# Latent attention in a macaron transformer kernel: the value products of a pair in two runs, with a ring of ten places for the exponents

## Chip, cores and metric

One Trainium2 chip (trn2), one core of it. The metric is the device time of the whole program in microseconds (us), as the median of several runs. All data are float32.

## What is computed

Input x has 4 batch elements of 1024 tokens with 128 channels. Six blocks follow each other, each on the layer norm of x and added to it: a mixture of experts (half weight), a causal attention with a polynomial in place of the softmax, the mixture of experts again, a feed-forward block with token-dependent weights, the latent attention, and the feed-forward block again. Only the latent attention is touched by the change. Cut to what matters:

```python
def _L1_attn_ref(x, latent_w, latent_b, Wd_w, Wd_b, out_w, out_b):
    b, t, c = x.shape                       # 4, 1024, 128
    Wdkv = x @ latent_w + latent_b          # keys and values alike, 36 wide
    q = jnp.einsum('btc,hcl->bhtl', x, Wd_w) + Wd_b[None, :, None, :]   # 16 heads
    scores = jnp.einsum('bhtl,bsl->bhts', q, Wdkv) / np.sqrt(8)
    scores = jnp.where(causal, scores, -jnp.inf)
    attn = jax.nn.softmax(scores, axis=-1)
    y = jnp.einsum('bhts,bsl->bhtl', attn, Wdkv)
    z = jnp.transpose(y, (0, 2, 1, 3)).reshape(b, t, h * 36)
    return z @ out_w + out_b
```

## The kernel before, in words

The function `attn1_phase` (from L1671) holds the latent attention. Each engine runs its own program, and semaphores alone order them against each other. `pipeline` (in each program: `start`, then four elements of eight `pair` calls and one `finish`) sets the order: an element is a batch element, a pair is two of the sixteen heads, m counts pairs over all elements, i counts them in an element, and q is i modulo 2. The first three elements run in a hardware loop with `more` true, the last one behind it with `more` false.

**Two passes over the scores.** The softmax needs the maximum of each row before the exponent. So the scores of a pair are computed twice. One pair ahead, `scores_max` (L1959) computes them with queries as rows, in sixteen blocks of 128 queries: eight wide ones (1024, 896, 768 or 640 keys) that all go to the same two PSUM banks, and eight narrow ones (512 keys or fewer) that all go to the third. VectorE's `maximum` (L2277) adds the causal mask to a block and takes the maximum of its rows; a small read instruction then ends it. Before TensorE writes a bank again it waits for the maximum of the block that lay there. The sixteen are dealt to slots 0 to 7 of TensorE's order (`MAXIMA`): one wide block in each, with narrow ones beside it. `transpose_max` (L1965) turns the sixteen maxima, ScalarE and VectorE split them in a high and a low part, and SP writes both to the query matrix with a small DMA each. Then the real `scores` (L1974) of the next pair, with keys as rows, can start: they wait for these DMAs (`m_in`).

**Units.** The real scores of a pair are computed in units. A unit holds for both heads (c = 0 and 1) a piece of 128 keys by up to 512 queries, or several smaller pieces. There are ten units, NU = 10: 0, 1 and 2 lie on the diagonal of the second half of the queries, 3 to 6 are full pieces of that half, 7, 8 and 9 are the diagonal of the first half. Units 0, 3 to 6 and 7 have 512 columns, 1 and 8 have 384 and 128, 2 and 9 have 256. A score matmul pair goes to one of three PSUM banks, ScalarE takes the exponent (L2174) into the tensor `probs`, GpSimd zeroes what lies above the diagonal in units 0, 1, 2, 7, 8 and 9 (L1886), and TensorE multiplies with the values (`values`, L1990) and adds up in one of two banks, one for each half of the queries. The value matmuls use 64 columns of the array for each head, so that both heads run side by side. `copy_out` on ScalarE (L2162) copies a finished half away.

**The ring.** `probs` has RING = 4 places of 1024 columns. Unit u of a pair lies at place (u + 2q) modulo 4 (`ring`, L1766). ScalarE's `exponent` waits ahead of a unit until the unit that lay four before in the order is multiplied (`pv_ready`, m * NU + u - RING).

**TensorE's order in a pair** is written by hand (L2033 to L2068), in STEPS = 5 steps d = 0 to 4. Each step has slot 2d - 1 of the maxima (from d = 1), three scores, slot 2d (up to d = 3), a fourth score, and then a run of value products: at d = 0 those of units 8 and 9 of the pair in front (if it belongs to the same element), at d = 1 units 0 and 1, at d = 2 units 2 and 3, at d = 3 units 4 and 5, at d = 4 units 6 and 7. At d = 4 the transpose of the maxima and `project` (the queries of the pair three further, L1943) stand ahead of the values. The last pair of an element has units 8 and 9 right behind 6 and 7. All of this is one queue: what stands behind a waiting instruction waits too.

**Special pairs.** Pair i = 5 (OPENS) of the first three elements transposes the next element's x in place of the projection. Pair i = 6, the opening pair, computes the next element's latents ahead of its first score, and at d = 0, behind the value products, projects queries (`project(m + 2, 0)`), for which ScalarE and VectorE then make the high and low parts, before slot 0 of the maxima. In the last element only pairs 0 to 4 project, and the last pair has no maxima.

**ScalarE's order in a pair** (`pair` at L2168 and on): the exponents of units 0 to 9, with `copy_out` of the second half of the pair in front behind unit 1, and in the opening pair `high_query` behind that; after the units the high part of the next queries, and the copy of the first half.

The order in the queues of SP and GpSimd is by `s_ready` (scores done), `qs_ready` and `p_ready` (exponents done); the change has no line there but for `ring`, which GpSimd's `causal_part` uses too.

Of the kernel before, what the change touches and what calls it, by code (L numbers as in the profile page):

```python
# [34 lines left out]
def after(n):  # L35

    return n + 1 + LEAD
# [1633 lines left out]
def attn1_phase(nc, t, tag):  # L1671


    with ExitStack() as ctx:
        def sb(name, shape, dt=F32):
            return ctx.enter_context(nc.sbuf_tensor(f"{tag}_{name}", shape, dt))
# [23 lines left out]
        ml = sb("ml", [16, 2, P], F32R)  # L1700
        probs = sb("probs", [P, RING, 2, HALF])
        yT = sb("yT", [P, PAIRS, SEQ])
# [31 lines left out]
        NU, NE = len(units), 2 * len(units)  # L1734
# [3 lines left out]
        STEPS = NU // 2  # L1738
# [26 lines left out]

        def ring(q, u):  # L1766

            return (u + 2 * q) % RING

        def o_part(j, rows, n):  # L1770

# [33 lines left out]
        def follows(i, k, more):  # L1805

            return more or i + k < PAIRS
# [5 lines left out]
        with nc.Block() as block:  # L1813
# [97 lines left out]
            def _(pe):  # L1911
# [35 lines left out]
                def scores_max(m, q, n, keys, spare=False):  # L1947
                    c, j = IN_ORDER[n]
                    before = bank_before(n, spare)
                    if not of_kind(n) and j >= 4:  # L1950
                        pe.wait_ge(q_in[q][0], (m - q) * 48 + 96)
                    elif not of_kind(n):
                        pe.wait_ge(q_in[q][1], (m - q) * 24 + 48)
                        pe.wait_ge(q_first[q], (m - q) * 24 + 48)
                    if before >= 0:
                        pe.wait_ge(mx_ready, after(m * 16 + before))
                    for lo in range(0, (j + 1) * P, HALF):
                        hi = min(lo + HALF, (j + 1) * P)
                        last = pe.matmul(max_part(n, lo, hi, spare), qS[q][0:STACK, c, j * P:(j + 1) * P], keys[0:STACK, lo:hi],  # L1959
                                         start=True, stop=True)  # L1960
                    last.then_inc(sm_ready, 1)

                def transpose_max(m, q):
                    pe.wait_ge(mx_ready, after(m * 16 + 15))
                    pe.transpose(o_part(0, 16, P), mx[:, q, :], t.ident).then_inc(mt_ready, 1)  # L1965
# [12 lines left out]
                def values(m, q, u):  # L1978
                    h = 0 if u < N1 else 1
                    pieces = units[u][1]  # L1980
                    first, end = u in (0, N1), u in (N1 - 1, NU - 1)
                    if first:
                        pe.wait_ge(yc_ready, after((m - 1) * 2 + h))
                    if u in DIAGONAL:
                        pe.wait_ge(tri_ready, after(m * len(DIAGONAL) + DIAGONAL.index(u)))
                    else:
                        pe.wait_ge(p_ready, after(m * NE + 2 * u + 1))
                    for k, (kt, at_, qc, n, _) in enumerate(pieces):
                        for c in range(2):
                            last = pe.matmul(y_bank[h][VW * c:VW * (c + 1), qc:qc + n], V[:, kt, :], probs[:, ring(q, u), c, at_:at_ + n],  # L1990
                                             start=first and k == 0, stop=end, skip_group_check=True)
                    last.then_inc(pv_ready, 1)
# [19 lines left out]
                def pair(m, i, b, more):  # L2012
                    q = i % 2
                    ahead = follows(i, 1, more)
                    opening = more and i == OPENS + 1
                    keys = kN if i == PAIRS - 1 else kS

                    def maximum(k):
                        if not ahead:
                            return  # L2020
                        if k == 0:
                            if follows(i, 2, more):
                                pe.wait_ge(qs_ready, after((m + 2) * 2 + 1))
                            pe.wait_ge(ml_ready, after(m))
                            if opening:
                                pe.wait_ge(v_ready, after(b + 1))
                        if k == 1 and i == 0:
                            pe.wait_ge(res.xo_ready, after(b * BT - 1))
                        for n in range(FIRST[k], FIRST[k + 1]):
                            scores_max(m + 1, 1 - q, n, keys)  # L2030

                    for d in range(STEPS):
                        if d == 0 and opening:  # L2033
                            latents(b + 1)
                        if d >= 1:
                            maximum(2 * d - 1)
                        for u, c in ((2 * d, 0), (2 * d, 1), (2 * d + 1, 0)):
                            scores(m, q, u, c)
                        if d == 0 and opening:
                            pe.wait_ge(ml_ready, after(m))  # L2040
                            latent_rows(b + 1)
                        if d < STEPS - 1 and not (d == 0 and opening):
                            maximum(2 * d)
                        scores(m, q, 2 * d + 1, 1)
                        if d == STEPS - 1:
                            if ahead:
                                transpose_max(m + 1, 1 - q)
                            if more and i == OPENS:
                                transpose_x(b + 1)
                            if projected(i, more):  # L2050
                                project(m + 3, (i + 3) % PAIRS)
                        if d == 0:
                            if i > 0:
                                for u in (NU - 2, NU - 1):
                                    values(m - 1, 1 - q, u)
                            if opening:
                                pe.wait_ge(ks_ready, after(b * 2 + 3))
                                project(m + 2, 0)
                                maximum(0)
                        else:  # L2060
                            for u in (2 * d - 2, 2 * d - 1):
                                values(m, q, u)
                    if i == PAIRS - 1:
                        for u in (NU - 2, NU - 1):
                            values(m, q, u)
# [47 lines left out]
            def _(act):  # L2113
# [44 lines left out]
                def copy_out(m, i, h):  # L2158
                    s = HALVES[h]
                    act.wait_ge(pv_ready, after(m * NU + (NU if h else N1) - 1))  # L2160
                    act.sem_inc(act_pause, 1)
                    act.activation(yT[:, i, s * HALF:(s + 1) * HALF], y_bank[h], ACT.Copy).then_inc(yc_ready, 1)  # L2162

                def pair(m, i, b, more):
                    q = i % 2
                    opening = more and i == OPENS + 1

                    def exponent(u, c):  # L2168
                        k = 2 * u + c
                        act.wait_ge(s_ready, after(m * NE + k))  # L2170
                        if c == 0:
                            act.wait_ge(pv_ready, after(m * NU + u - RING))
                        n = 256 if len(units[u][1]) == 1 and units[u][1][0][3] == 256 else HALF
                        act.activation(probs[:, ring(q, u), c, HALF - n:HALF], e_part(k, HALF - n, HALF), ACT.Exp,  # L2174
                                       scale=SCORE_SCALE).then_inc(p_ready, 1)

                    if opening:
                        low_keys(b + 1)
                    for u in range(NU):
                        exponent(u, 0)  # L2180
                        if u == NU - 1 and follows(i, 1, more):
                            high_max(m + 1, 1 - q)
                        exponent(u, 1)
                        if u == 1:
                            if i > 0:
                                copy_out(m - 1, i - 1, 1)
                            if opening:
                                high_query(m + 2, 0, True)
                    if more and i == OPENS:
                        high_x(b + 1)  # L2190
                    if projected(i, more):
                        high_query(m + 3, (i + 3) % PAIRS, True)
                    copy_out(m, i, 0)
                    if i == PAIRS - 1:
                        copy_out(m, i, 1)
# [125 lines left out]
        sem.end()  # L2321


RING = 4
OPENS = PAIRS - 3


# [127 lines left out]
```

## Time and profile before

| | us |
|---|---|
| median of 3 runs | 3007.7 (3005.54 to 3011.52) |
| the profiled execution, its time | 3009.96 |
| its span in the trace | 3008.2 |
| TensorE matmul busy | 2717.3 (90%) |
| VectorE busy | 1908.3 (63%) |
| ScalarE busy | 1136.8 (38%) |
| GpSimd busy | 924.1 (31%) |
| mean granted TensorE clock | 0.937 of full speed |

Busy time is the union of an engine's instruction spans, and matmul ends are modelled, so a TensorE that is busy in the table is not one at its peak. The latent attention fills the span from about 2010 to 2915 us; an ordinary pair takes about 23 us of it.

### The profile page before, as it was taken

The page shows a single profiled execution, that of the slowest core. Times are in us where ns is not written, and L with a number is a line of the kernel's source. Part 1 is how long each engine was busy: PE and PEld are TensorE (multiplying, and loading weights), DVE is VectorE, ACT ScalarE, POOL GpSimd, SP SyncE. Part 2 cuts the span into 40 slices and gives each one's busy share as a digit, 9 for nine tenths or more (in the row PEclk, how much of TensorE's full clock was granted, in tenths as well). Part 3 has the DMA queues.
Part 4 walks back from the last instruction along what each step waited for, and adds up shares of the span by engine and source line. Part 5 has one row for each costly group of instructions (what it writes and reads, how often), then busy time and mean ns, then how long its engine had stood idle before and what let it go on. Part 6 is the DMA issues. An engine that isn't in the chain of part 4 may idle for free. (4 is left out here: it accounts for less than half of the span.)

```text
span 3008.2 us, 53420 instructions
## 1 busy us (share of the span) xinstructions
PE 2717.3 (90%) x15208; PEld 1878.1 (62%) x15208; DVE 1908.3 (63%) x5011; ACT 1136.8 (38%) x2101; POOL 924.1 (31%) x1235
## 2 busy tenths in 40 slices
PE   6999999968888888789999999778998998998989
PEld 5888888845555555468888888434455455455454
DVE  6777777746665666477777777445555555555542
ACT  3111111116666667521111111234544544544544
POOL 3222233216666666542222222001111211211200
PEclk9999999968898898889999999888999999999999
DMA  4000000000000000110000000001111111111100
GB/s 138 0 0 0 0 0 0 0 1 2 2 3 3 3 3 3 36 67 0 0 0 0 0 0 1 1 21 28 43 31 28 43 30 28 43 29 31 43 2 28
DMA packets 31963, 51.87 MB, mean 17 GB/s; under 512 B 8178, under 2 KB 14066, under 8 KB 31732
## 3 DMA queue, kind: packets, MB, share of 16 engines
q1 hardware_dynamic: 27124, 41.88, 4.6%
q0 software_dynamic: 4608, 7.09, 0.9%
q8 instruction: 124, 2.03, 0.3%
q14 instruction: 107, 0.88, 0.1%
HBM read 17.93 MB, written 2.10 MB: 7 GB/s over the span
## 5 line engine op out<-in xcount | busy, mean ns | idle before, releaser
L640 DVE SCALAR_TENSOR_TENSOR moe_acc<-moe_ps,moe_comb,moe_acc 128x512 f32<-128x512 f32 x896 | 660.9, 744 | 154.5 <-PE moe_ps L346 151.5
L2277 DVE CUSTOM_DVE_ANT_0 attn_masked<-attn_psm,attn_causal 128x1024 f32<-128x1024 f32 (+1 forms) x504 | 363.2, 757 | 260.4 <-PE attn_psm L1959 259.7
L2174 ACT ACTIVATE attn_probs<-attn_pse 128x512 f32<-128x512 f32 (+1 forms) x640 | 313.6, 556 | 342.4 <-PE attn_pse L1974 339.8
L377 PE MATMUL moe_ps<-moe_Wd,moe_ih 128*128 128x512 f32 x1024 | 344.1, 418 | 4.6 <-DVE moe_Wd L563 4.6
L346 PE MATMUL moe_ps<-moe_Wg,moe_xh 128*128 128x512 f32 x1024 | 328.9, 403 | 16.9 <-DVE moe_Wg L563 16.9
L346 PE MATMUL moe_ps<-moe_Wu,moe_xh 128*128 128x512 f32 x1024 | 334.1, 408 | 2.7 <-POOL moe_Wu L501 2.7
L1886 POOL TENSOR_SCALAR_AFFINE_SELECT attn_probs<-attn_probs 128x256 f32<-128x256 f32 (+1 forms) x192 | 95.1, 496 | 711.9 <-ACT attn_probs L2174 711.8
L1990 PE MATMUL attn_psy<-attn_probs,attn_V 128*64 128x512 f32 (+3 forms) x1536 | 291.4, 510 | 0.0
L511 POOL TENSOR_SCALAR moe_part<-consts,moe_pick,moe_prob 128x8 f32<-128x8 f32 x256 | 97.9, 400 | 626.9 <-ACT moe_prob L434 626.9
L1959 PE MATMUL attn_psm<-attn_kS,attn_qS 108*128 108x512 f32 (+3 forms) x672 | 197.8, 395 | 49.9 <-DVE attn_mx L2277 43.9
L1145 POOL TENSOR_TENSOR attn_R<-attn_R 128x1024 f32<-128x1024 f32 (+1 forms) x128 | 213.9, 1681 | 92.5 <-DVE attn_R L1511 91.7
L346 PEld LDWEIGHTS moe_ps<-moe_Wg,moe_xh 128*128 128x128 f32 x1024 | 195.2, 192 | 65.7 <-issue 20.8
L1974 PE MATMUL attn_pse<-attn_qS,attn_kS 110*128 110x512 f32 (+3 forms) x768 | 207.5, 366 | 23.3 <-ACT attn_probs L2174 10.3
L346 PEld LDWEIGHTS moe_ps<-moe_Wu,moe_xh 128*128 128x128 f32 x1024 | 191.3, 192 | 47.0 <-issue 5.4
L1959 PEld LDWEIGHTS attn_psm<-attn_kS,attn_qS 108*128 108x128 f32 x672 | 112.5, 195 | 168.0 <-DVE attn_mx L2277 147.4
L433 ACT ACTIVATE moe_prob<-moe_gap 128x2 f32<-128x2 f32 x64 | 13.0, 203 | 519.4 <-DVE moe_gap L631 519.4
L377 PEld LDWEIGHTS moe_ps<-moe_Wd,moe_ih 128*128 128x128 f32 x1024 | 182.8, 193 | 41.0 <-issue 4.8
L346 PE MATMUL moe_ps<-moe_Wg,moe_xl 128*128 128x512 f32 x512 | 205.2, 401 | 0.0
L346 PE MATMUL moe_ps<-moe_Wu,moe_xl 128*128 128x512 f32 x512 | 204.8, 400 | 0.0
L377 PE MATMUL moe_ps<-moe_Wd,moe_il 128*128 128x512 f32 x512 | 203.6, 398 | 0.0
L1511 DVE TENSOR_SCALAR attn_R<-attn_e 128x1024 f32<-128x1024 f32 (+1 forms) x128 | 139.2, 1087 | 92.9 <-PE attn_e L1210 87.1
L1990 PEld LDWEIGHTS attn_psy<-attn_probs,attn_V 128*64 128x64 f32 x1536 | 97.0, 140 | 134.7 <-issue 122.9
(233 smaller groups left out, 4686.9 us busy)
## 6 DMA issues: line engine op xcount, KB each, us to landing
attn_qS<-attn_qH SPq DMA_DIRECT2D x192, 72.0 KB
attn_qS<-attn_qL SPq DMA_DIRECT2D x96, 72.0 KB
attn_qS<-attn_qH POOLq DMA_DIRECT2D x64, 72.0 KB, 2.0
moe_stageg<-in_w_gate SPq DMA_DIRECT2D x8, 512.0 KB, 7.2
moe_stageu<-in_w_up SPq DMA_DIRECT2D x8, 512.0 KB, 7.4
moe_stageg<-in_w_down SPq DMA_DIRECT2D x8, 512.0 KB, 4.0
attn_qS<-attn_qL POOLq DMA_DIRECT2D x32, 72.0 KB, 2.5
out<-X SPq DMA_DIRECT2D x8, 256.0 KB, 2.4
```

The source lines that it names most:

```text
L346: last = pe.matmul(expert_bank[j % 4][:, :], a[q][:, :], w[b][:, cols], start=k == 0, stop=k == 2)
L377: last = pe.matmul(y_bank[h][:, :], a[q][:, rows], W[2][b][:, cols], start=c == 0 and k == 0, stop=c == KC - 1 and k == 2)
L511: ins = pool.tensor_scalar(part[:, q, r, k, :], t.iota8, pick[:, q, r, k:k + 1], prob[:, q, r, k:k + 1], ALU.is_equal, ALU.mult)
L640: dve.scalar_tensor_tensor(acc[:, q, r, :], expert_bank[j % 4][:, :], comb[:, q, r, e:e + 1], acc[:, q, r, :], ALU.mult, ALU.add).then_inc ...
L1145: pool.tensor_tensor(r, r, r, ALU.mult).then_inc(sq01_ready, 1)
L1511: dve.tensor_scalar(R[:, r, 0:2, HALF - n:HALF], e01[u % 2][:, :, HALF - n:HALF], LIFT, -HALF_LIFT, ALU.max, ALU.add).then_inc(read01, 1)
L1886: pool.affine_select(some, some, [[0, 2], [0, (hi - lo) // P], [1, P]], ALU.is_ge, nothing, base=0, channel_multiplier=-1).then_inc(tri_re ...
L1959: last = pe.matmul(max_part(n, lo, hi, spare), qS[q][0:STACK, c, j * P:(j + 1) * P], keys[0:STACK, lo:hi], start=True, stop=True)
L1974: last = pe.matmul(e_part(k, at_, at_ + n), kS[:, kt * P:(kt + 1) * P], qS[q][:, c, s * HALF + qc:s * HALF + qc + n], start=True, stop=True)
L1990: last = pe.matmul(y_bank[h][VW * c:VW * (c + 1), qc:qc + n], V[:, kt, :], probs[:, ring(q, u), c, at_:at_ + n], start=first and k == 0, s ...
L2174: act.activation(probs[:, ring(q, u), c, HALF - n:HALF], e_part(k, HALF - n, HALF), ACT.Exp, scale=SCORE_SCALE).then_inc(p_ready, 1)
L2277: dve.tensor_tensor_reduce(masked[:, 0 if j >= 4 else 1, 0:n], max_part(k, 0, n, spare), causal[:, SEQ - n:SEQ], 1.0, NEG, ALU.add, ALU.ma ...
```

## The change

The value products of a pair come in two runs. The first, at d = 1, has units 8 and 9 of the pair in front and then units 0 and 1. The second, at the end of d = 4, has units 2 to 7. Steps 0, 2 and 3 have none. The last pair of an element still has units 8 and 9 at its end. Since exponents now wait longer for their product, the ring has ten places, one for each unit, and a unit lies at the place of its own number. On ScalarE the copy of the second half of the pair in front moves from behind unit 1 to behind unit 3.

```diff
         def ring(q, u):
 
-            return (u + 2 * q) % RING
+            return u
...
-                        if d == 0:
+                        if d == 1:
                             if i > 0:
                                 for u in (NU - 2, NU - 1):
                                     values(m - 1, 1 - q, u)
+                            for u in range(2):
+                                values(m, q, u)
+                        if d == STEPS - 1:
+                            for u in range(2, NU - 2):
+                                values(m, q, u)
+                        if d == 0:
                             if opening:
                                 pe.wait_ge(ks_ready, after(b * 2 + 3))
                                 project(m + 2, 0)
                                 maximum(0)
-                        else:
-                            for u in (2 * d - 2, 2 * d - 1):
-                                values(m, q, u)
...
                         exponent(u, 1)
+                        if u == 3 and i > 0:
+                            copy_out(m - 1, i - 1, 1)
                         if u == 1:
-                            if i > 0:
-                                copy_out(m - 1, i - 1, 1)
                             if opening:
                                 high_query(m + 2, 0, True)
...
-RING = 4
+RING = 10
```

## Rows read from the trace of the kernel before

In the order of time the columns are: start us, us, engine, line, operation, output<-inputs, xcount, and in brackets the idle time before it and its releaser; instructions of a kind are merged, and overlapping groups may start before the one in front ends. In the stretches the columns are: start:end, length, busy us (xcount) of PE, PEld, DVE, ACT and POOL, granted clock, DMA share, GB/s.

**Rows 1.** The order of time, TensorE, one ordinary pair (columns as above).

```profile
2337.80 0.96 PE L1974 MATMUL attn_pse<-attn_qS,attn_kS 110*128 110x512 f32 x4 [0.17 <-DMA attn_qS<-attn_ml]
...
2339.50 1.51 PE L1990 MATMUL attn_psy<-attn_probs,attn_V 128*64 128x384 f32 x12
2340.95 0.84 PE L1959 MATMUL attn_psm<-attn_kS,attn_qS 108*128 108x512 f32 x3
...
2342.80 1.12 PE L1959 MATMUL attn_psm<-attn_kS,attn_qS 108*128 108x512 f32 x3 [0.55 <-DVE attn_mx L2277]
...
2347.24 0.44 PE L1959 MATMUL attn_psm<-attn_kS,attn_qS 108*128 108x384 f32 x1 [0.49 <-DVE attn_mx L2277]
2347.51 0.87 PE L1974 MATMUL attn_pse<-attn_qS,attn_kS 110*128 110x512 f32 x3
2348.22 0.76 PE L1959 MATMUL attn_psm<-attn_kS,attn_qS 108*128 108x512 f32 x3
2348.82 0.39 PE L1974 MATMUL attn_pse<-attn_qS,attn_kS 110*128 110x512 f32 x1
2349.14 1.51 PE L1990 MATMUL attn_psy<-attn_probs,attn_V 128*64 128x256 f32 x8
2350.58 0.73 PE L1959 MATMUL attn_psm<-attn_kS,attn_qS 108*128 108x512 f32 x3
...
2352.24 0.73 PE L1959 MATMUL attn_psm<-attn_kS,attn_qS 108*128 108x512 f32 x3 [0.22 <-DVE attn_mx L2277]
...
2353.18 1.94 PE L1990 MATMUL attn_psy<-attn_probs,attn_V 128*64 128x512 f32 x8
2355.05 0.67 PE L1959 MATMUL attn_psm<-attn_kS,attn_qS 108*128 108x512 f32 x3
...
2356.77 0.38 PE L1974 MATMUL attn_pse<-attn_qS,attn_kS 110*128 110x256 f32 x1 [0.31 <-ACT attn_probs L2174]
...
2358.89 1.94 PE L1990 MATMUL attn_psy<-attn_probs,attn_V 128*64 128x512 f32 x8
2361.17 0.96 PE L1974 MATMUL attn_pse<-attn_qS,attn_kS 110*128 110x512 f32 x4 [0.34 <-DMA attn_qS<-attn_ml]
```

**Rows 2.** The same stretch, VectorE: the reads that end four wide maxima.

```profile
2340.69 0.08 DVE L2277 DVE_READ_ACCUMULATOR2_ANT attn_mx<- 128x1 f32 x1
...
2350.02 0.08 DVE L2277 DVE_READ_ACCUMULATOR2_ANT attn_mx<- 128x1 f32 x1
...
2352.10 0.08 DVE L2277 DVE_READ_ACCUMULATOR2_ANT attn_mx<- 128x1 f32 x1
...
2354.15 0.08 DVE L2277 DVE_READ_ACCUMULATOR2_ANT attn_mx<- 128x1 f32 x1
```

**Rows 3.** The order of time, TensorE: an opening pair and a first pair.

```profile
2193.22 0.71 PE L1959 MATMUL attn_psm<-attn_kS,attn_qS 108*128 108x512 f32 x2 [1.88 <-DVE attn_qL L2253]
2195.50 0.84 PE L1959 MATMUL attn_psm<-attn_kS,attn_qS 108*128 108x512 f32 x3 [1.57 <-DVE attn_mx L2277]
...
2270.82 1.43 PE L1959 MATMUL attn_psm<-attn_kS,attn_qS 108*128 108x512 f32 x3 [1.55 <-DVE attn_mx L2277]
```

**Rows 4.** The same view: the run at the end of an element.

```profile
2238.63 3.23 PE L1990 MATMUL attn_psy<-attn_probs,attn_V 128*64 128x512 f32 x20
2241.80 1.09 PE L2079 MATMUL attn_psm<-consts,attn_yT 128*128 128x128 f32 x8
```

**Rows 5.** The order of time, TensorE: the last element, starts of pairs 6 and 7.

```profile
2852.21 0.96 PE L1974 MATMUL attn_pse<-attn_qS,attn_kS 110*128 110x512 f32 x4 [1.17 <-DMA attn_qS<-attn_ml]
...
2875.77 0.96 PE L1974 MATMUL attn_pse<-attn_qS,attn_kS 110*128 110x512 f32 x4 [2.12 <-DMA attn_qS<-attn_ml]
```

**Rows 6.** Stretches: the opening pairs of the first two elements.

```profile
2184.52:2217.81 33.29, 28.35 (x134) 15.75 (x133) 16.63 (x40) 14.85 (x29) 4.49 (x9) 0.90 0.09 25
2408.26:2443.14 34.88, 29.99 (x134) 16.65 (x133) 16.64 (x40) 14.88 (x29) 4.49 (x9) 0.85 0.09 24
```

**Rows 7.** The order of time, ScalarE, in the pair of rows 1.

```profile
2348.03 2.06 ACT L2174 ACTIVATE attn_probs<-attn_pse 128x512 f32<-128x512 f32 x4 [3.25 <-PE attn_pse L1974]
```

## The prediction

> **What bounds the kernel now.** I read the attention part of the second layer, since the diff touches nothing else. I went first to the order of time on TensorE, pair by pair, then to VectorE in the same stretch, then to the stretches with their granted clock. One pair of heads is the stretch from its first score matmul to that of the next, 2337.80 to 2361.17, 23.37 us [rows 1]. Within it TensorE never stands for long. Its marked waits are 0.55 and 0.49 and 0.22 us (for VectorE's maxima), 0.31 (an exponent) and 0.34 (the DMA of the low part of the maxima) [rows 1]. So TensorE's stream sets the end, but only because of how it is interleaved. Slot after slot it writes a block of masked scores for the next pair into the one wide bank, VectorE takes its maximum, and TensorE must not write the wide bank again until VectorE has read it. The value products (L1990) are what TensorE does in the meantime: five runs, at d = 0 to 4. Three of them lie exactly on such a wait [rows 1, 2]:
> - The run of units 8 and 9 goes from 2339.50 to 2340.95. VectorE's read of the 1024-wide block ends at 2340.69 + 0.08 = 2340.77.
> - The run of units 2 and 3 goes from 2349.14 to 2350.58. The read of the 896-wide block ends at 2350.10.
> - The run of units 4 and 5 goes from 2353.18 to 2355.05. The read of the second 896-wide block ends at 2354.23.
> How soon TensorE follows such a read: the one ending at 2352.10 + 0.08 = 2352.18 is followed by a matmul at 2352.24, 0.06 us later [rows 1, 2].
>
> What happens without a run as cover is also shown. The first pair of an element has no run at d = 0, and TensorE waits 1.55 us there (2270.82). The opening pair has its run ahead of the first maximum, not behind it, and waits 1.57 us at the same place (2195.50) [rows 3].
>
> **The change, part by part.** Values of 8 and 9 move from d = 0 to d = 1, those of 2 to 5 move from d = 2 and 3 to the end of d = 4. No matmul is added or dropped. I work out one ordinary pair.
>
> *What a run costs when it is joined to another.* Alone, units 6 and 7 (the same shapes as 4 and 5) take 2355.05 - 2353.18 = 1.87 and units 8 and 9 take 1.45, together 3.32. As one run at the end of an element they take 2241.80 - 2238.63 = 3.17 [rows 1, 4]. Joining saves 0.15. Further, the score ahead of a run takes 0.32 (2348.82 to 2349.14), and scores among themselves (2348.22 - 2347.51)/3 = 0.24. That is 0.08 more. So a run less saves 0.23, plus whatever the first matmul after a run loses, which I leave at nothing because after a wait it is lost as well. The moved work then costs, in its new place: 8 and 9, 1.45 - 0.15 = 1.30; 2 and 3, 1.44 - 0.15 = 1.29; 4 and 5, 1.87 - 0.15 = 1.72. Sum 4.31 us.
>
> *What leaving the old places gives.* There the next wide block can start 0.06 after the read of the last: at 2340.83 instead of 2340.95 (0.12), at 2350.16 instead of 2350.58 (0.42), at 2354.29 instead of 2355.05 (0.76). Sum 1.30 us. The rest becomes waiting: about 1.3 us at d = 0, 1.0 at d = 2, 1.1 at d = 3. The 0.08 ahead of each run only makes that wait longer.
>
> *The end of a pair.* The next pair's first score waits for the two small DMAs with the maxima, which start from the transpose at L1965. Here 2.28 us pass from the start of the last run (2358.89) to that score (2361.17), where a run of this size takes 1.87, so 0.41 waits. The trace marks 0.34 of it as a wait, and 0.17 ahead of this pair's own first score (2337.80), so I take the mean, 0.25. With six units in that run instead of two it is 3 us longer and the wait is gone. That is the change's one sure gain.
>
> Ordinary pair: 4.31 - 1.30 - 0.25 = **+2.76 us**. There are 16 (pairs 1 to 4 of the four elements): 44.2.
> - Pairs 5 and 7 of the first three elements have no such DMA wait at their end to win (latent products or transposes follow): 4.31 - 1.30 = 3.01, six times, 18.1.
> - Opening pair (6) of three elements: without 8 and 9 at d = 0 its projection comes 1.45 sooner, and the queries' chain through ScalarE and VectorE, for which TensorE waits 1.88 at 2193.22 [rows 3], moves with it. -1.45 + 1.30 + (1.29 + 1.72 - 0.42 - 0.76 - 0.25) = 1.43, 4.3 in all.
> - Pair 0 has no values of a pair in front: only the last bracket, 1.58, four times, 6.3.
> - Last element, pairs 5 and 6: no projection, so the DMA wait is larger, 1.17 and 2.12 [rows 5], and the longer run covers it: 3.01 - 1.17 = 1.84 and 3.01 - 2.12 = 0.89, together 2.7.
> - The last pair has no maxima. The exponents pace it, and the stream of values is merely taken later: 0.
> Sum **75.6 us**.
>
> *The clock.* The granted clock falls from its upper level (2.4 GHz) to its lower (1.2 GHz) where waits lie close together, as the 1.88 and 1.57 us of the opening pair do [rows 3, 6]. The two opening pairs in [rows 6] are alike but for this: 34.88 us at a mean of 0.85 against 33.29 at 0.90, so 3.4 us more at the low level cost 1.6 us. The new waits at d = 0 and d = 1 (1.3 and the 0.55 that stays, about a microsecond apart) are less than those of the opening pair and far more than any in today's ordinary pair. Bounds: no fall, 0; a fall in each of the 24 pairs with such a place (16, 6 and 2 of the list), 38 us. I take about a third, 8 falls, 13 us, since the sum of the two is nearer to the opening pair's than to nothing. Estimated from rows of this trace.
>
> The Trainium skill bears on this (TensorE: Matmul & The Clock Gate, section "A second HAM failure mode: psum-queue depth-cycling"): small idles of TensorE between groups of matmuls can be frequent enough that the clock gate goes back and forth. By that page alone I would take the upper bound of 38 us instead of 13, a forecast 25 us higher. The trace agrees that idles bring the low level [rows 3, 6]; that waits as short as the new ones do it in every pair, it does not show.
>
> *The rest, at nothing.* The ring of ten places makes an exponent wait for the same unit of the pair in front; for 8 and 9 that product stands at d = 1, long before their exponents at d = 4. Room in SBUF grows only. ScalarE's copy of the second output half moves from behind unit 1 to behind unit 3, since it must now wait for the values at d = 1. It covers itself: ScalarE sits idle 3.25 us ahead of the exponents of units 4 and 5 (2348.03) [rows 7], and an operation on 512 columns takes it some 0.5 us (four in 2.06). Left in its old place it would have held up the exponents of units 2 and 3, for which the scores and so the values themselves wait. The queues of SP and POOL are not reordered: their queries and selects go by the scores and exponents. At the end of a pair the copy of the first half (0.6 us) comes when unit 6 is done. In the new run one unit follows it, 0.9 us, so it ends about when the next pair's first score starts, ahead of its first exponent. If that cover failed it would cost up to 0.5 us a pair.
>
> The profiled execution took 3009.96 us: 3009.96 + 75.6 + 13 = 3098.6. The median of the runs is 2.3 lower, so I forecast **3096 us**, 2.9% slower.
>
> **Rivals.**
> 1. *The runs were no cover* (other side: faster). If VectorE's part of the chain also came sooner when TensorE is freed, or if those reads ended earlier than the rows say, the waits would not open and only the saved starts would count: 92 runs fewer (3 in each of 28 pairs, 2 in each first one) at 0.23 is 21, and the DMA waits 0.25 x 23 + 1.17 + 2.12 = 9. 3007.7 - 30 = 2978. It decides if the open waits come to less than about 0.9 us a pair. Against it: VectorE starts each maximum right after the matmuls, and the 1.55 and 1.57 [rows 3] are such open waits. Chance 0.06. The Trainium skill's rule speaks for this side (TensorEngine Tiling (Array Packing), section "Key Properties": changing the tiling mode drains TensorE, and the value products use halves of 64 columns). The trace agrees that there is a price, a few tenths, but not that it decides.
> 2. *The clock falls in every pair*: 75.6 + 38, so 3121. For it: waits of 1.0 to 1.3 us three times a pair. Against: long full runs lie between. Chance 0.16.
> 3. *Something else fills the places* (VectorE's narrow maxima and the exponents are spread so that only the 2.76 shrinks to a microsecond or less), 28 us or less, 3036. Chance 0.08; with a part of it, 0.04, inside 6 us of no change.
> The change not doing what it says I hold for out: the moved calls are plain calls in the written order of TensorE. Forecast: 0.66.
>
> **Numbers.** 0.2%, about 6 us, is what a measurement can tell from no change. The likeliest case spans 75 us with no fall of the clock to 38 us more, and the terms read from one pair may be off by a tenth: 3075 to 3129. To take in most of rivals 2 and 3 the range goes to **3050 to 3138**, leaving out rival 1 and the mild end of 3. Slower 0.90, same 0.04, faster 0.06.
>
> **What would show it.** In the profile of the changed kernel: a pair of 25.5 to 26.5 us; TensorE waits for the maxima of about 1.3 us at d = 0, 1.0 at d = 2, 1.1 at d = 3 with values out of sight; no DMA wait ahead of a pair's first score; one run of about 3.1 us and one of about 4.7 us; total waits of TensorE on the maxima up by some 80 us; more stretches at the lower clock. It would be wrong if a pair stays at 23 us or the waits do not open.

## The result, and the profile after

The changed kernel takes 3161.72 us (median of 4 runs, 3158.98 to 3164.52), against 3008.36 us for the kernel before (median of 4 runs) beside it. The ratio is 1.0508, with a 95% interval of 1.049 to 1.0526: 153 us slower. The forecast was slower, by 88 us. The direction held, and the measured time lies outside the range of 3050 to 3138.

Lines of the profile page after: the span, TensorE's busy time, and its granted clock in forty slices.

```profile
span 3161.8 us, 53420 instructions
...
PE 2795.7 (88%) x15208; PEld 1935.7 (61%) x15208; DVE 1909.6 (60%) x5011; ACT 1140.4 (36%) x2101; POOL 925.0 (29%) x1235
...
PEclk9999999968888898799999998788889888898889
```

TensorE is 78 us busier than before (2717.3 then) with the same 15208 matmuls, and in the last fifteen slices, most of them the latent attention, eleven of the digits of the clock are 8, where before three are. The mean granted clock of the whole program went from 0.937 to 0.906. With two levels only, 1.0 and 0.5, that is 2 x 0.063 x 3008 = 379 us at the low level before and 2 x 0.094 x 3162 = 594 us after. I use this figure, "low time", for every run below. It is that of one profiled execution; among the executions of one kernel it differs by 10 to 40 us.

Who waited for whom, total us, times, longest; first the kernel before, then the changed one. PEld is the weight load, PE the matmul.

```profile
PEld attn_psm L1959 <- DVE attn_mx L2277: 163.7, 273, 2.0
...
PE attn_psm L1959 <- DVE attn_mx L2277: 47.9, 100, 1.9
```

```profile
PEld attn_psm L1959 <- DVE attn_mx L2280: 218.4, 271, 2.3
...
PE attn_psm L1959 <- DVE attn_mx L2280: 137.3, 179, 1.9
```

TensorE's matmul waits on VectorE's maxima went up by 89 us, those of the weight load by 55. The waits on the small DMA ahead of a pair (`attn_qS<-attn_ml`) are gone from the list.

The order of time on TensorE in a pair after the change in which the clock stayed up. It answers to [rows 1].

```profile
2073.57 0.97 PE L1974 MATMUL attn_pse<-attn_qS,attn_kS 110*128 110x512 f32 x4
...
2076.64 0.85 PE L1959 MATMUL attn_psm<-attn_kS,attn_qS 108*128 108x512 f32 x3 [1.29 <-DVE attn_mx L2280]
...
2078.49 1.11 PE L1959 MATMUL attn_psm<-attn_kS,attn_qS 108*128 108x512 f32 x3 [0.54 <-DVE attn_mx L2280]
...
2079.77 3.24 PE L1990 MATMUL attn_psy<-attn_probs,attn_V 128*64 128x384 f32 x24
2082.94 0.79 PE L1959 MATMUL attn_psm<-attn_kS,attn_qS 108*128 108x384 f32 x3
2084.22 0.45 PE L1959 MATMUL attn_psm<-attn_kS,attn_qS 108*128 108x384 f32 x1 [0.49 <-DVE attn_mx L2280]
...
2087.16 0.73 PE L1959 MATMUL attn_psm<-attn_kS,attn_qS 108*128 108x512 f32 x3 [0.96 <-DVE attn_mx L2280]
...
2088.82 0.74 PE L1959 MATMUL attn_psm<-attn_kS,attn_qS 108*128 108x512 f32 x3 [0.23 <-DVE attn_mx L2280]
...
2090.87 0.68 PE L1959 MATMUL attn_psm<-attn_kS,attn_qS 108*128 108x512 f32 x3 [1.03 <-DVE attn_mx L2280]
...
2094.39 4.94 PE L1990 MATMUL attn_psy<-attn_probs,attn_V 128*64 128x256 f32 x24
2099.27 0.96 PE L1974 MATMUL attn_pse<-attn_qS,attn_kS 110*128 110x512 f32 x4
```

The places where the value products stood now show as waits: 1.29 us at d = 0 (2076.64), 0.96 at d = 2 (2087.16), 1.03 at d = 3 (2090.87). The 0.54, 0.49 and 0.23 that stood before are still there. The first run goes from 2079.77 to 2082.94, the second from 2094.39 to 2099.27, and the next score follows it without a wait.

Stretches after the change (columns as in the stretches before): all pairs from the second to the start of the last, a pair without a fall of the clock, two pairs with, and three parts of the first of those two.

```profile
2073.57:3028.13 954.56, 799.75 (x3746) 471.24 (x3744) 460.86 (x1253) 398.53 (x806) 137.82 (x273) 0.87 0.11 28
2073.57:2099.26 25.69, 20.84 (x105) 11.50 (x103) 13.32 (x35) 12.47 (x25) 4.50 (x9) 1.00 0.13 36
2334.17:2363.99 29.82, 25.32 (x105) 14.02 (x103) 13.32 (x35) 12.60 (x25) 4.51 (x9) 0.83 0.12 31
...
2339.54:2342.95 3.41, 3.41 (x16) 1.73 (x16) 1.94 (x6) 0.61 (x2) 0.11 (x1) 0.53 0.00 0
2342.95:2353.19 10.24, 7.54 (x38) 4.44 (x35) 5.85 (x18) 4.83 (x9) 0.42 (x1) 0.99 0.06 16
2353.19:2360.02 6.83, 6.83 (x22) 4.24 (x23) 2.60 (x7) 3.26 (x7) 2.60 (x5) 0.52 0.33 89
...
2363.99:2394.38 30.39, 25.50 (x105) 13.80 (x103) 13.32 (x35) 12.50 (x25) 4.50 (x9) 0.83 0.11 30
```

The same for the kernel before: all pairs in the same sense, and one pair.

```profile
2067.93:2875.76 807.83, 730.05 (x3744) 419.37 (x3744) 459.83 (x1253) 395.28 (x806) 137.50 (x273) 0.97 0.13 34
2067.93:2090.83 22.90, 21.18 (x103) 11.21 (x103) 13.33 (x35) 12.36 (x25) 4.49 (x9) 1.00 0.15 40
```

A pair without a fall is 25.69 us long, where the one that answers to it before is 22.90: 2.79 us more. The pairs with falls are 29.82 and 30.39. In the pair that starts at 2334.17 the clock is low twice: from 2339.54 for 3.4 us and from 2353.19 for 6.8 us. What TensorE did ahead of each (and, in the first list, the run that then went at the low clock):

```profile
2337.22 0.85 PE L1959 MATMUL attn_psm<-attn_kS,attn_qS 108*128 108x512 f32 x3 [1.26 <-DVE attn_mx L2280]
...
2339.08 1.48 PE L1959 MATMUL attn_psm<-attn_kS,attn_qS 108*128 108x512 f32 x3 [0.54 <-DVE attn_mx L2280]
...
2340.92 4.11 PE L1990 MATMUL attn_psy<-attn_probs,attn_V 128*64 128x384 f32 x24
2344.95 0.79 PE L1959 MATMUL attn_psm<-attn_kS,attn_qS 108*128 108x384 f32 x3
```

```profile
2350.82 0.74 PE L1959 MATMUL attn_psm<-attn_kS,attn_qS 108*128 108x512 f32 x3 [0.22 <-DVE attn_mx L2280]
...
2352.87 1.07 PE L1959 MATMUL attn_psm<-attn_kS,attn_qS 108*128 108x512 f32 x3 [1.03 <-DVE attn_mx L2280]
```

The first fall comes right behind d = 0's wait (1.26 us) and the 0.54 of the next slot, and the run of value products at 2340.92 then takes 4.03 us instead of 3.17. The second comes behind the waits of d = 2 to 4, of which 0.22 and 1.03 stand here.

### The profile page after: what moved, and what is told of

It reads as the page before. It is cut to its first block and busy times, and to the rows that moved or that the text cites. A ratio compares the mean times of both kernels' runs of the same rounds, so it can differ in the third digit from the quotient of the medians.

```text
span 3161.8 us, 53420 instructions
## 1 busy us (share of the span) xinstructions
PE 2795.7 (88%) x15208; PEld 1935.7 (61%) x15208; DVE 1909.6 (60%) x5011; ACT 1140.4 (36%) x2101; POOL 925.0 (29%) x1235
## 5 line engine op out<-in xcount | busy, mean ns | idle before, releaser
L1959 PE MATMUL attn_psm<-attn_kS,attn_qS 108*128 108x512 f32 (+3 forms) x672 | 211.0, 419 | 129.5 <-DVE attn_mx L2280 123.5
L1959 PEld LDWEIGHTS attn_psm<-attn_kS,attn_qS 108*128 108x128 f32 x672 | 121.0, 208 | 217.9 <-DVE attn_mx L2280 195.8
L1974 PE MATMUL attn_pse<-attn_qS,attn_kS 110*128 110x512 f32 (+3 forms) x768 | 226.5, 395 | 11.9 <-issue 6.0
L1990 PEld LDWEIGHTS attn_psy<-attn_probs,attn_V 128*64 128x64 f32 x1536 | 114.4, 155 | 180.4 <-issue 173.5
```

Of the source, the lines that this page charges most:

```text
L1974: last = pe.matmul(e_part(k, at_, at_ + n), kS[:, kt * P:(kt + 1) * P], qS[q][:, c, s * HALF + qc:s * HALF + qc + n], start=True, stop=True)
```

## The experiments

Each result is set against the kernel before, measured again beside it (median 3009.54 us for e1 to e4, 3006.18 for e5 to e8, 3007.57 for e9 and e10).

| run | median us | against before | mean clock | low time |
|---|---|---|---|---|
| before | 3008.36 | | 0.937 | 379 |
| changed | 3161.72 | +153.4 | 0.906 | 594 |
| e1 ring only | 3009.68 | +0.1 | 0.937 | 379 |
| e2 8 and 9 moved | 3052.45 | +42.9 | 0.930 | 427 |
| e3 2 to 5 moved | 3102.95 | +93.4 | 0.920 | 496 |
| e4 changed, filler 5, 4, 4 | 3077.39 | +67.9 | 0.941 | 363 |
| e5 changed, filler at d = 0 | 3128.69 | +122.5 | 0.917 | 519 |
| e6 changed, filler at d = 2, 3 | 3102.52 | +96.3 | 0.930 | 433 |
| e7 before with filler | 2993.31 | -12.9 | 0.943 | 341 |
| e8 reordered runs | 3001.52 | -4.7 | 0.936 | 384 |
| e9 e8 and filler | 2988.39 | -19.2 | 0.943 | 341 |
| e10 changed, filler 3, 2, 2 | 3082.13 | +74.6 | 0.941 | 363 |

**The ring alone.** Before, with the ring of the change.

```diff
-            return (u + 2 * q) % RING
+            return u
...
-RING = 4
+RING = 10
```

> The kernel before with the ring of ten places alone (unit u at place u), every run of value products and the copy where they were. Theory A (the ring only takes room): 3008 us, within 6 us of before, ordinary pairs of 23.2 us. Theory B (the larger ring itself costs, by the addresses or the longer wait on the products): a good part of the 153 us shows here, 3030 us or more.

Measured: 3009.68 us, ratio 1.0001 (0.9988 to 1.0013). The ring costs nothing. Theory B is out.

**One half of the change each.** The changed kernel with units 2 to 7 in their old runs:

```diff
-                            for u in range(2):
-                                values(m, q, u)
-                        if d == STEPS - 1:
-                            for u in range(2, NU - 2):
+                        if d >= 1:
+                            for u in (2 * d - 2, 2 * d - 1):
                                 values(m, q, u)
```

> Only the values of units 8 and 9 move to d = 1; units 2 to 7 stay in their old runs. Theory A (lost cover, then the clock): 24 pairs lose 1.18 us of cover, 28 us, and the waits of 1.3 and 0.55 us near each other bring the low clock in part of the pairs, 10 to 50 us more: 3045 to 3085 us, with pairs without a fall at 24.1 to 24.4 us. Theory B (cover alone; the clock costs only what I had forecast): 3035 to 3042 us.

And with 8 and 9 (and the copy on ScalarE) in their old place:

```diff
+                        if d == 0 and i > 0:
+                            for u in (NU - 2, NU - 1):
+                                values(m - 1, 1 - q, u)
                         if d == 1:
-                            if i > 0:
-                                for u in (NU - 2, NU - 1):
-                                    values(m - 1, 1 - q, u)
...
-                        if u == 3 and i > 0:
+                        if u == 1 and i > 0:
                             copy_out(m - 1, i - 1, 1)
```

> Only the values of units 2 to 5 move to the end of d = 4; units 8 and 9 stay at d = 0. Theory A (lost cover, then the clock): 1.58 us in an ordinary pair, 48 us over the phase, and the waits of 1.0, 0.2 and 1.0 us at d = 2 to 4 bring falls of their own, 20 to 60 us more: 3075 to 3115 us, with pairs without a fall at about 24.8 us. Theory B (these waits are too far apart for the clock): 3056 us with the clock of this phase as before.

Measured: 3052.45 (ratio 1.0152, 1.0134 to 1.017) and 3102.95 (1.0323, 1.0303 to 1.0344). Both are what theory A gave, and both have more low time than before, by 48 and 117 us. So both halves bring the clock down, and the later places (d = 2 to 4), where the prediction had no fall, do so more. Together the two halves lose 136 of the 153 us.

**Work added in the opened waits.** The decisive run. At the end of a step TensorE does score matmuls of 512 columns whose output the next score overwrites. They wait for nothing that the next score doesn't wait for.

```diff
+                    def filler(u, n):
+                        if not ahead:
+                            return
+                        k = 2 * u
+                        pe.wait_ge(p_ready, after(m * NE + k - 3))
+                        for _ in range(n):
+                            pe.matmul(e_part(k, 0, HALF), kS[:, 0:P], qS[q][:, 0, 0:HALF], start=True, stop=True)
...
+                        if d in {0: 5, 2: 4, 3: 4}:
+                            filler(2 * d + 2, {0: 5, 2: 4, 3: 4}[d])
```

> The changed kernel with useless score matmuls of 512 columns, 5 at the end of d = 0 and 4 at the end of d = 2 and of d = 3, written to the bank that the next score overwrites: they fill the opened waits on VectorE without taking the place of anything, so they can't shorten a wait. Theory A (half of the 153 us is the clock): the clock stays up, ordinary pairs 25.6 to 26.0 us throughout, 3085 to 3095 us, although 13 matmuls a pair are added. Theory B (the extra time lies in waits and in the longer runs, and the clock follows from it): 3155 us or more.

Measured: 3077.39 us, ratio to before 1.0228 (1.0209 to 1.0247). Thirteen useless matmuls in each of 31 pairs (the very last has no maxima and gets none) make the changed kernel 84 us faster. Its stretches, all pairs and one pair:

```profile
2068.89:2944.03 875.14, 806.90 (x4136) 492.05 (x4134) 459.81 (x1253) 395.69 (x806) 137.95 (x273) 0.99 0.12 31
2313.64:2339.32 25.68, 24.00 (x118) 13.69 (x116) 13.32 (x35) 12.47 (x25) 4.51 (x9) 1.00 0.13 36
```

And TensorE's order of time, where the filler (L2038) stands ahead of the next wide block:

```profile
2096.33 1.43 PE L2038 MATMUL attn_pse<-attn_qS,attn_kS 110*128 110x512 f32 x5
2097.97 0.86 PE L1959 MATMUL attn_psm<-attn_kS,attn_qS 108*128 108x512 f32 x3 [0.21 <-DVE attn_mx L2290]
...
2107.49 1.20 PE L2038 MATMUL attn_pse<-attn_qS,attn_kS 110*128 110x512 f32 x4
2108.52 0.70 PE L1959 MATMUL attn_psm<-attn_kS,attn_qS 108*128 108x512 f32 x3
...
2111.02 1.09 PE L2038 MATMUL attn_pse<-attn_qS,attn_kS 110*128 110x512 f32 x4
2112.21 0.67 PE L1959 MATMUL attn_psm<-attn_kS,attn_qS 108*128 108x512 f32 x3
```

Nothing waits longer for VectorE at these places than 0.21 us, the pair is 25.68 us long, as the undisturbed pair of the changed kernel, and its clock is 1.00. The filler took no time of its own and gave back no wait. What it took away is the low clock: 231 us less of it for 84 us, 0.365 us for each us. My expectation of 3085 to 3095 was some 8 us too high. The pairs have even less low time than before (0.99 against 0.97 in the stretches of all pairs), which it had not counted: 24 us against 44 in these stretches, by the clock's records, so some 7 us.

**Which place.** The same filler at d = 0 alone (`{0: 5}`), and at d = 2 and 3 alone (`{2: 4, 3: 4}`).

> The changed kernel with filler matmuls at the end of d = 0 alone (5 of 512 columns), none at d = 2 and 3. The clock theory: the waits at d = 2 and 3 bring falls of their own (with units 2 to 5 alone moved the phase had 122 us more at the low level), those at d = 0 fewer (44 us more with 8 and 9 alone moved). So most of the loss stays: 3110 to 3140 us. If one place alone sets off the falls and it is d = 0: 3077 to 3090 us.

> The changed kernel with filler matmuls at the end of d = 2 and d = 3 alone (4 each), none at d = 0. The clock theory: 3090 to 3115 us, the better of the two halves, with some 110 to 130 us at the low level in the phase. If d = 0 is what sets off the falls: 3140 us or more.

Measured: 3128.69 (1.0402, 1.0386 to 1.0418) and 3102.52 (1.0327, 1.031 to 1.0344), both as the clock theory had it. Filling d = 0 alone brings 33 us, filling the later two alone 59, both at once 84: d = 0 and the later two each set off falls of their own. Between d = 2 and d = 3 no run tells.

**How much must be filled.** 3, 2 and 2 matmuls in place of 5, 4 and 4.

> The changed kernel with 3, 2 and 2 filler matmuls at d = 0, 2 and 3 in place of 5, 4 and 4, so that some 0.5 to 0.7 us of each opened wait stays open. The clock theory says that what counts is how much TensorE idles within a few microseconds, not whether each wait is filled: nearly all of the gain, 3077 to 3090 us. If the waits must be filled whole: about half of it, 3110 to 3130 us.

Measured: 3082.13 (1.0251, 1.0229 to 1.0272), 5 us from the full filler. A wait need not be filled: two or three matmuls of 0.24 us in each bring nearly all of the gain. In its trace 0.69 us stay open at d = 0 (2333.20), 0.28 at d = 2 (2317.67) and 0.56 at d = 3 (2321.39). The low time in the table is that of its fastest execution, 3076.91 us; the mean of its four is 382, so a few more falls than with the full filler are left.

**Back to the kernel before.** If idle TensorE time costs by the clock, the waits of the kernel before in its opening pairs [rows 3] do so too.

```diff
                                 project(m + 2, 0)
+                                filler(7)
                                 maximum(0)
+                                filler(6)
+                            elif i == 0:
+                                filler(3)
```

> The kernel before with filler matmuls only where it waits long itself: 7 ahead of slot 0 and 6 behind it in the opening pair, 3 at the end of d = 0 in the first pair of an element. The clock theory: the low stretches of the three opening pairs (6.8 to 10.2 us each) go in good part and those of the first pairs shorten, 5 to 15 us in all, 2995 to 3004 us. The rival that the clock falls from something else there: 3009 us or up to 5 us more.

Measured: 2993.31 us, ratio 0.9959 (0.9946 to 0.9973), 12.9 us faster than before, inside the 5 to 15 us that were expected (the time itself is 2 us under its range, since the kernel before was 3006.18 us here). Its three opening pairs have 3.4 us at the low clock each, where the kernel before has 6.8, 10.2 and 10.2.

**Runs cut closer to their wait.** Before with the ring of ten, and:

```diff
-                            for u in (2 * d - 2, 2 * d - 1):
+                            for u in ((0, 1), (3,), (2, 4), (5, 6, 7))[d - 1]:
                                 values(m, q, u)
```

> The kernel before with the ring of ten, which frees the order of the units: runs 8, 9 at d = 0, units 0, 1 at d = 1, unit 3 at d = 2, units 2, 4 at d = 3, units 5, 6, 7 at d = 4. Each run then just fills its wait (1.0 us at d = 2, 1.4 at d = 3, where before had 1.44 and 1.87) and the last one covers the DMA wait. By the rows: -0.42 - 0.43 + 0.86 - 0.25 = -0.24 us an ordinary pair, and some 0.9 us in pairs 5 and 6 of the last element: 3001 to 3005 us. Rival (cover cut too close, the clock falls more often): 3010 us or more.

Measured: 3001.52 us, ratio 0.9986 (0.9977 to 0.9995), 4.7 us faster. In its order of time the next wide block follows the two middle runs at 2349.12 and 2353.18 without a marked wait. VectorE's reads of the wide maxima end at 2349.06 and 2352.78, so the first run just fills its wait and the second still ends 0.4 us after it, where before it ended 0.8 after (2354.23 and 2355.05).

```profile
2348.10 1.08 PE L1990 MATMUL attn_psy<-attn_probs,attn_V 128*64 128x512 f32 x4
2349.12 0.74 PE L1959 MATMUL attn_psm<-attn_kS,attn_qS 108*128 108x512 f32 x3
...
2351.74 1.51 PE L1990 MATMUL attn_psy<-attn_probs,attn_V 128*64 128x256 f32 x8
2353.18 0.67 PE L1959 MATMUL attn_psm<-attn_kS,attn_qS 108*128 108x512 f32 x3
...
2357.03 2.80 PE L1990 MATMUL attn_psy<-attn_probs,attn_V 128*64 128x512 f32 x12
2359.75 0.51 PE L1974 MATMUL attn_pse<-attn_qS,attn_kS 110*128 110x512 f32 x1
```

**Both.**

> The two gains together: the reordered runs (3, then 2 and 4, then 5 to 7, ring of ten) and the filler matmuls in the opening pair and the first pair. They touch different places, so they should add up: 3006 - 4.7 - 12.9, 2988 us, 2983 to 2993. Rival (the longer last run already did a part of what the filler does): 2992 us or more.

Measured: 2988.39 us, ratio 0.9927 (0.991 to 0.9944). The two gains add up, and this version beats both kernels. Its opening pair, the stretch and the two fillers (L2035) in it:

```profile
2180.79:2211.29 30.50, 28.48 (x147) 17.00 (x145) 16.63 (x40) 14.78 (x29) 4.48 (x9) 1.00 0.10 26
```

```profile
2187.45 1.80 PE L2035 MATMUL attn_pse<-attn_qS,attn_kS 110*128 110x512 f32 x7
2189.49 0.70 PE L1959 MATMUL attn_psm<-attn_kS,attn_qS 108*128 108x512 f32 x2 [0.24 <-DVE attn_qL L2262]
2190.04 1.54 PE L2035 MATMUL attn_pse<-attn_qS,attn_kS 110*128 110x512 f32 x6
2191.77 0.84 PE L1959 MATMUL attn_psm<-attn_kS,attn_qS 108*128 108x512 f32 x3 [0.19 <-DVE attn_mx L2286]
```

It is 30.50 us long with the clock at 1.00 throughout; before had 33.29 and 34.88 at 0.90 and 0.85 [rows 6]. The waits of 1.88 and 1.57 [rows 3] are 0.24 and 0.19.

## Why the prediction was right in direction and wrong in size

- *The runs were cover, and their work costs again where it is moved*: right. It stands in the pair without a fall: runs of 3.17 and 4.88 us, which are the prediction's 1.30 + 1.87 and 1.29 + 1.72 + 1.87 to the hundredth; waits of 1.29, 0.96 and 1.03 where about 1.3, 1.0 and 1.1 were forecast; the DMA wait at the end gone. Forecast +2.76 us, measured +2.79.
- *The sum of 75.6 us over the phase*: right. The filler run e4 shows it without the clock, since 24 of its 31 pairs (all but the opening ones and the first of each element) have 1 us of low time among them, and the same pairs of the kernel before have none. Pair 5 of the first element and pair 6 of the last, first before and then in e4 (columns as in the stretches):

```profile
2160.37:2184.52 24.15, 22.44 (x111) 12.41 (x112) 15.19 (x43) 12.45 (x26) 4.50 (x9) 1.00 0.15 43
2852.21:2875.77 23.56, 19.95 (x98) 10.47 (x98) 11.92 (x33) 11.06 (x23) 2.96 (x6) 1.00 0.05 13
```

```profile
2172.31:2199.46 27.15, 25.29 (x126) 14.93 (x125) 15.19 (x43) 12.47 (x26) 4.51 (x9) 1.00 0.13 35
2919.64:2944.03 24.39, 22.80 (x112) 12.99 (x110) 11.92 (x33) 11.05 (x23) 2.97 (x6) 1.00 0.01 4
```

They are 3.00 and 0.83 us longer, where 3.01 and 0.89 were forecast. All 24 together are 66.8 us longer, where the sum had 44.2 + 18.1 + 2.7 = 65.0. The other seven, forecast at 4.3 + 6.3 us, have low time in one of the two kernels or in both, and can't be read so. Over the whole program, 215 us more of low time at 0.365 are 78 us, and 153 - 78 = 75 are left; that fits, but it is no second witness, since the 0.365 comes from e4 too. The halves, priced in the same way, come out at 43 - 17.5 = 25 and 93 - 43 = 51, where the rows gave 27.9 (the moved 8 and 9) and 47.7.
- *The clock*: this is the term that failed. It was put at 8 falls of 3.4 us, 1.6 us each, 13 us, with 38 as the upper bound. It is 78 us. I counted only the place at d = 0 and 1 and called the waits of d = 2 to 4 nothing, where the experiments give them the larger part. I took one fall of 3.4 us as the size, 27 us of low time in eight; 22 of the 24 pairs that I had listed have low time, 3.4 to 13.7 us each, 165 us in all. The stretches of the opening pairs could have told me, since by their clock they already had 6.7 and 10.5 us of it (2 x 0.10 x 33.29 and 2 x 0.15 x 34.88) [rows 6]. I left out the three opening and four first pairs, which have 93 us after against 56 before. So the upper bound of one fall in each of 24 pairs was no bound. Nor did a third of these pairs follow from its reason: a sum of waits nearer to that of the opening pair than to nothing speaks for more than half. The price itself was near: the 1.6 us for 3.4 us read from the two opening pairs is 0.47 us for each us, and 0.365 was measured over the program, 0.39 in the 24 pairs (63.4 us between the changed kernel and e4, for 164 us). That it isn't 0.5 I put down to the waits on VectorE, which shrink while TensorE is slow. No run took this apart.
- *The rivals*: the fall in every pair was the right mechanism (29 of the 31 pairs ahead of the last have low time), given 0.16 and, with one fall of 3.4 us in each, only 3121 us. The faster side ("the runs were no cover") has nothing left: TensorE's waits opened as forecast. Joining runs did save, as the sum had it.
- *The last pair at nothing*: off. The first line is from the kernel before and gives the end of that pair's value products, the others are from the changed one:

```profile
2893.46 1.09 PE L2079 MATMUL attn_psm<-consts,attn_yT 128*128 128x128 f32 x8
```

```profile
3028.13 0.96 PE L1974 MATMUL attn_pse<-attn_qS,attn_kS 110*128 110x512 f32 x4
...
3047.50 1.09 PE L2082 MATMUL attn_psm<-consts,attn_yT 128*128 128x128 f32 x8
```

From the first score, 2875.77 [rows 5], that was 17.69 us, and now it is 19.37. It is a pair without maxima, and the clock was low for 3.4 us in it, from 3039.03 on, ahead of its run of eight units and into it. It is 1.7 us, once.
- *The ring, the copy, the queues at nothing*: right for the ring (e1). The copy was only tried together with the moved values of 8 and 9 (e2).

The Trainium skill's rule that I had weighed at 25 us more (TensorE: Matmul & The Clock Gate, section "A second HAM failure mode: psum-queue depth-cycling") was the better guide: the clock gate does go back and forth with small idles between groups of matmuls, 594 us of low time against 379. The 38 us that I would have taken by it are still half of the 78 measured. Here it is the falls themselves that the filler takes away.

## What to carry to other kernels

Work of TensorE that stands between its own output and another engine's read of it is cover: before it is gathered into longer runs for the sake of a few tenths per start, see in the order of time what wait each piece lies on, and move only what is longer than its wait. Then price the clock apart from the waits, for every place that opens, and don't cap it at one fall for each; waits of 1 us that recur can cost as much again as the time they take. Where such a wait can't be closed, matmuls whose output is overwritten can pay: they did here, by 84 and by 13 us.

## What the runs showed of the hardware that I had not expected

- TensorE's granted clock fell to its low level although no single wait in the pair was longer than 1.3 us and TensorE was busy for 25.3 of 29.8 us by the profile (which counts the half-rate matmuls as busy). In the pair without a fall it was busy 20.8 of 25.7 us, with the same waits: whether a pair has a fall is not told by its own pattern alone.
- Useless matmuls made a kernel faster: by 84 us in the changed kernel, which with them is still 68 us slower than the kernel before, and by 13 us in the kernel before.
- A microsecond at the low clock cost 0.365 us by the profiled executions (0.37 by the mean clocks of all of them), not half a microsecond, in a loop in which TensorE also waits for VectorE.
